# Half the staged writes, eight strided fetches a pair, and output projections behind the attention loop

## Chip, core and metric

The kernel runs on one core of one Trainium2 chip. The metric is the device time of one execution in microseconds (us), lower being better. TensorE (PE) multiplies matrices, VectorE (DVE), ScalarE (ACT) and GpSimd (POOL) work element by element, and SyncE (SP) issues the DMAs.

## What is computed

One macaron block on x of shape (2, 1024, 128), all in fp32: half of a routed feed-forward network (FFN, 8 experts of width 512, two per token), attention with 16 heads (key width 16, value width 64), and half of the FFN again, each behind a layer norm and added to x. The attention's softmax runs over the queries (axis 1), not over the keys.

```python
def _L0_attn_ref(x, query_proj, key_proj, value_proj, output_proj):
    q = jnp.einsum('bnd,hkd->bnhk', x, query_proj)
    k = jnp.einsum('bnd,hkd->bnhk', x, key_proj)
    v = jnp.einsum('bnd,hvd->bnhv', x, value_proj)
    sim = jnp.einsum('bnkh,bmhk->bnhm', q, k)
    attn = jax.nn.softmax(sim * scale, axis=1)
    o = jnp.einsum('bnhm,bmhv->bnhv', attn, v)
    return jnp.einsum('bnhv,dhv->bnd', o, output_proj)

x = x + 0.5 * _L0_ffn_ref(_layernorm(x), ...)
x = x + _L0_attn_ref(_layernorm(x), ...)
x = x + 0.5 * _L0_ffn_ref(_layernorm(x), ...)
```

`_L0_ffn_ref` takes a softmax over 8 router logits, keeps the two largest, and sums gelu(x W1 + b1) W2 + b2 over all experts with these weights.

## The kernel before

The 2048 tokens lie as 16 tiles of 128, in four groups of four tiles. Each engine has its own instruction list, written by hand; semaphores join them. For precision most matmuls take operands split in a high and a low part (three matmuls for one product), the split being made by a copy and a subtraction. A matmul on plain fp32 operands is recorded as two passes in the trace.

**FFN** (`ffn_pe`, `ffn_act`, `ffn_dve`, `ffn_pool`, `ffn_sync`). All eight experts run over all tokens, in four iterations `i` of two experts; an iteration has eight units `s`, one expert and one token group each. On TensorE `hidden(i, s + 1)` (lines 358 to 360) goes ahead of `output(i, s)` (369 to 371). ACT (`front`) applies gelu, DVE (`front`) makes the high and low parts (621, 625) and evicts the output block times its gate into `ysc`, a ring of two (`back`, 648), and POOL (`add`, 481) sums it into `acc`. In the first iteration the router runs on DVE: `router()` is a generator of 20 small linked steps, some of them laid between the passes of units 2 and 3; its result is transposed by TensorE into bank 5 (399) and copied by DVE (692), and TensorE holds the fourth output block until then. In the last iteration `back_pe` (170) transposes a finished token group of `acc` back, when POOL has summed its last expert, and `residual_dve` (177) adds it to x.

**Staging** (`queries`, `values` in `att_pe`; `high_part`, `low_part`; `stage`, `load_pair` on SP). Queries and keys come out of 16 units (query or key, one of two groups of eight heads, one token group). ACT writes the high part into `sthi`, DVE the low part into `stlo`, both rings of four, and SP writes them to a DRAM buffer (823). A score matmul wants four 16-row blocks a head: query parts (high, high, low, low) against key parts (high, low, high, low). The buffer has four blocks a head, so `stage` writes each part twice, and `load_pair(k)` fetches the query and the key side of two heads with one DMA of 128 rows each (813). `high_part(n)` waits until unit n - 4 is written out. `load_pair(0)` stands on SP behind units 0 to 7.

**Attention loop** (`products`, `scores`, `maxima`, `exps`, `inverses`). 16 pairs of heads (8 for each batch), eight steps of 128 keys for each pair. A step has score matmuls (896) five heads ahead, negated maxima on DVE (1067), exponentials on ACT (1002), values scaled on POOL, and products (910) into banks 6 and 7. In the second batch's eight pairs, one of batch 0's eight output-projection tiles stands between the two halves of the first step's products: `outproj` (917) into bank 7, then `residual` on DVE (1085), and the second half waits for that. Batch 1's projections are groups 2 and 3 behind the loop, inside `first()` of the second FFN.

## Time and profile before

| | us |
|---|---|
| median of 3 runs (819.36 to 821.10) | 820.52 |
| profiled execution | 819.94 |
| its span on the core | 818.1 |
| TensorE busy | 780.2 (95%) |
| DVE busy | 677.1 (83%) |
| ACT busy | 617.4 (75%) |
| POOL busy | 202.8 (25%) |

The span is the time from the first to the last recorded instruction; the rest of the execution lies around it. A busy TensorE says only that its matmuls overlap without a gap, so the places to look at are stretches in which it waits, and work that it could be spared. The first FFN runs to about 203 us, staging to 262, the loop from there to 606, and the second FFN from there to the end.

### The profile page before, as it was taken

The numbers are of one execution on the slowest core, as the hardware profiler recorded it, in microseconds if no ns is written. First come the engines' busy times: TensorE is split into PE (matmuls) and PEld (weight loads), VectorE is DVE, ScalarE is ACT, GpSimd is POOL, SyncE is SP. The second block draws the span as 40 slices with busy tenths as digits, with TensorE's granted clock in tenths as the row PEclk, the third lists the DMA queues.
The fourth block names the chain that finished last, engine by engine and source line by source line (L and its number), as shares of the span: only waits on it lengthen the run. The fifth ranks groups of instructions, "written<-read, shape, count | busy, mean of one in ns | idle before, by whom it ended". The sixth has DMA issues, their size and how long they took to land.

```text
span 818.1 us, 11781 instructions
## 1 busy us (share of the span) xinstructions
PE 780.2 (95%) x3626; PEld 464.3 (57%) x3626; DVE 677.1 (83%) x1353; ACT 617.4 (75%) x1018; POOL 202.8 (25%) x263
## 2 busy tenths in 40 slices
PE   7999999998948999999999999999999999999996
PEld 5778888886724333333333333333349678888885
DVE  7778888878727999999999888888875878888886
ACT  4867777765725999999998888888864767777762
POOL 3116532334200111111111111211121117333322
PEclk8999999999988999999999999999999999999999
DMA  5041213110798111111311110011000042202111
GB/s 171 1 158 51 104 52 103 53 52 0 276 328 322 51 52 52 52 52 52 104 52 52 52 44 24 36 52 52 1 2 1 4 155 94 99 20 97 52 51 52
DMA packets 29509, 63.04 MB, mean 77 GB/s; under 512 B 5264, under 2 KB 10768, under 8 KB 27408
## 3 DMA queue, kind: packets, MB, share of 16 engines
q1 hardware_dynamic: 29456, 62.39, 21.7%
q8 instruction: 27, 0.44, 0.2%
q14 instruction: 26, 0.21, 0.1%
HBM read 44.42 MB, written 17.96 MB: 76 GB/s over the span
## 4 chain that ended last, share of the span: by engine, by line
PE 82%; DVE 6%; DMA 5%; SPq 3%; ACT 2%; issue 1%; POOL 1%; POOLq 0%; DVEq 0%; ACTq 0%
PE ps L910 29%; PE ps L896 10%; PE ps L358 6%; PE ps L359 6%; PE ps L360 6%; PE ps L370 6%; PE ps L369 6%; PE ps L371 6%; PE ps L917 4%; SPq L823 2%; DMA w2raw<-in_w 2%; DMA qk_parts<-stlo 2%; DVE hlo L625 2%; POOL acc L481 1%; DVE hhi L621 1%
## 5 line engine op out<-in xcount | busy, mean ns | idle before, releaser
L1067 DVE TENSOR_SCALAR_CACHE_REDUCE ef<-ps 128x1024 f32<-128x1024 f32 x256 | 308.5, 1215 | 22.8 <-PE ps L896 15.4
L1002 ACT ACTIVATE ef<-ef,nmax 128x1024 f32<-128x1024 f32 x256 | 294.4, 1150 | 26.9 <-DVE ef L1067 19.5
L910 PE MATMUL ps<-ef,vs 128*64 128x512 f32 x1024 | 249.5, 605 | 3.9 <-DVE xt L1085 3.8
L435 ACT ACTIVATE ps<-ps,b_sb 128x512 f32<-128x512 f32 x256 | 169.1, 663 | 102.5 <-PE ps L360 100.5
L625 DVE TENSOR_TENSOR hlo<-ps,hhi 128x512 fp32r<-128x512 f32 x256 | 165.5, 686 | 4.8 <-ACT ps L435 0.7
L1113 POOL TENSOR_TENSOR vs<-V,rsum 128x128 f32<-128x128 f32 x128 | 51.4, 401 | 332.8 <-DVE rsum L1073 332.8
L910 PEld LDWEIGHTS ps<-ef,vs 128*64 128x64 f32 x1024 | 62.1, 136 | 120.7 <-issue 109.4
L621 DVE CAST hhi<-ps 128x512 fp32r<-128x512 f32 x128 | 87.6, 685 | 50.0 <-ACT ps L435 50.0
L481 POOL TENSOR_TENSOR acc<-acc,ysc 128x512 f32<-128x512 f32 x56 | 72.0, 1289 | 155.4 <-DVE ysc L648 154.8
L358 PE MATMUL ps<-xhi,w1lo 128*128 128x512 f32 x256 | 103.4, 404 | 3.5 <-DVE hlo L625 3.5
L359 PE MATMUL ps<-xlo,w1hi 128*128 128x512 f32 x256 | 101.8, 398 | 0.0
L360 PE MATMUL ps<-xhi,w1hi 128*128 128x512 f32 x256 | 101.8, 397 | 0.0
L369 PE MATMUL ps<-hhi,w2lo 128*128 128x512 f32 x256 | 100.8, 394 | 0.8 <-DVE gT L692 0.8
L370 PE MATMUL ps<-hlo,w2hi 128*128 128x512 f32 x256 | 100.2, 391 | 0.0
L371 PE MATMUL ps<-hhi,w2hi 128*128 128x512 f32 x256 | 99.8, 390 | 0.0
L896 PEld LDWEIGHTS ps<-qs,ks 64*128 64x128 f32 x512 | 38.6, 184 | 105.1 <-DVE ef L1067 96.2
L896 PE MATMUL ps<-qs,ks 64*128 64x512 f32 x512 | 94.9, 444 | 1.9 <-DVE ef L1067 1.9
L434 ACT ACTIVATE hhi<-ps,b_sb 128x512 fp32r<-128x512 f32 x128 | 88.6, 692 | 6.2 <-PE ps L360 1.5
L358 PEld LDWEIGHTS ps<-xhi,w1lo 128*128 128x128 f32 x256 | 48.5, 190 | 18.6 <-DVE hlo L625 7.0
L360 PEld LDWEIGHTS ps<-xhi,w1hi 128*128 128x128 f32 x256 | 48.5, 189 | 11.9
L369 PEld LDWEIGHTS ps<-hhi,w2lo 128*128 128x128 f32 x256 | 48.0, 188 | 12.2 <-DVE gT L692 1.5
L359 PEld LDWEIGHTS ps<-xlo,w1hi 128*128 128x128 f32 x256 | 48.5, 190 | 10.8
(95 smaller groups left out, 675.3 us busy)
## 6 DMA issues: line engine op xcount, KB each, us to landing
gb<-gates SPq DMA_DIRECT2D x16, 1024.0 KB, 4.6
qk_parts<-sthi SPq DMA_DIRECT2D x32, 256.0 KB, 3.6
qk_parts<-stlo SPq DMA_DIRECT2D x32, 256.0 KB, 3.9
qs<-qk_parts SPq DMA_DIRECT2D x16, 512.0 KB, 4.2
ks<-qk_parts SPq DMA_DIRECT2D x16, 512.0 KB, 5.2
w1raw<-in_w SPq DMA_DIRECT2D x16, 256.0 KB, 5.1
w2raw<-in_w SPq DMA_DIRECT2D x16, 256.0 KB, 5.5
xt<-in_x SPq DMA_DIRECT2D x4, 256.0 KB, 4.5
```

The lines of the kernel that those rows point to most:

```text
L358: nc.tensor.matmul(bank(mc), w1lo[:, u, w], xhi[:, cols], start=True, stop=False)
L359: nc.tensor.matmul(bank(mc), w1hi[:, u, w], xlo[:, cols], start=False, stop=False)
L360: nc.tensor.matmul(bank(mc), w1hi[:, u, w], xhi[:, cols], start=False, stop=True).then_inc(F.h, 1)
L369: nc.tensor.matmul(y, w2lo[:, u, w], hhi[:, s % 2, mc, :], start=(mc == 0), stop=False)
L370: nc.tensor.matmul(y, w2hi[:, u, w], hlo[:, s % 2, mc, :], start=False, stop=False)
L371: last = nc.tensor.matmul(y, w2hi[:, u, w], hhi[:, s % 2, mc, :], start=False, stop=(mc == MC - 1))
L435: nc.scalar.activation(bank(mc), bank(mc), ACT.Gelu, bias=b1_sb[:, u, mc:mc + 1]).then_inc(F.gelu, 1)
L625: nc.vector.tensor_tensor(hlo[:, s % 2, mc, :], bank(mc), hhi[:, s % 2, mc, :].bitcast(F32), ALU.subtract).then_inc(F.lo, 1)
L896: last = nc.tensor.matmul(bank(slot_bank(u) + half), ks[rows, k % 2, m * P:(m + 1) * P], qs[rows, k % 2, half * 512:(half + 1) * 512], sta ...
L910: last = nc.tensor.matmul(bank(6 + half)[x * VD:(x + 1) * VD, :], vs[:, t % VRING, x * VD:(x + 1) * VD], ef[:, (2 * t + x) % ERING, half * ...
L1002: nc.scalar.activation(ef[:, c, :], ef[:, c, :], ACT.Exp, scale=-1.0, bias=nmax[:, c:c + 1], accum_out=esum[:, c:c + 1]).then_inc(s_exp, 1)
L1067: nc.vector.tensor_scalar(ef[:, c, :], bank(slot_bank(u), 2), -1.0, None, ALU.mult, ALU.min, accum_out=nmax[:, c:c + 1]).then_inc(s_max, 1)
```

## The change

1. **Staging.** The DRAM buffer holds two blocks a head instead of four; each part is written once, and the copy is made by the fetch: `load_pair` issues eight DMAs of 32 rows, each into every fourth partition, instead of two of 128 rows. `load_pair(0)` moves behind units 8 and 9, and the written-out semaphores are kept for each batch apart.
2. **Output projections.** Batch 0's tiles leave the loop and become groups 0 and 1 behind it, in banks 4 and 5. Their residuals and statistics move there too.
3. **Ends of the last expert.** DVE evicts output blocks 1, 2 and 3 one unit earlier. In the first FFN, the forward transpose of group 0 goes ahead of the last output block on TensorE.
4. **Router.** Links are laid into unit 3 alone; unit 2 goes ahead of them, one eviction between them, and ACT does unit 3 ahead of the exponential.
5. **Last sum.** For the last token group TensorE adds `acc` and `ysc` in PSUM (`finish_pe`) instead of POOL.

```diff
-        qkd = nc.dram_tensor("qk_parts", [2, H, KD, 4, TOK], F32, kind="Internal").ap()
+        qkd = nc.dram_tensor("qk_parts", [2, H, KD, 2, TOK], F32, kind="Internal").ap()
...
+        def finish_pe(pe, n, g):
+            F = ffns[1]
+            pe.wait_ge(F.acc, A0 + GR * (E - 3) + g + 1)
+            for t in range(TPG):
+                at = (g * TPG + t) * P
+                nc.tensor.matmul(bank(back_bank(n, g))[:, t * P:(t + 1) * P], acc[:, at:at + P], ident, start=True, stop=False)
+                if t == 0:
+                    pe.wait_ge(F.scaled, S0 + GR * E)
+                last = nc.tensor.matmul(bank(back_bank(n, g))[:, t * P:(t + 1) * P], ysc[:, (2 * GR - 1) % 2, t * P:(t + 1) * P],
+                                        ident, start=False, stop=True)
+            last.then_inc(n.back, 1)
...
             def first():
-                forward_pe(pe, n, 0)
-                forward_pe(pe, n, 1)
                 if outproj:
+                    outproj(0)
+                    outproj(1)
+                    forward_pe(pe, n, 0)
+                    pe.wait_ge(n.res, 1)
                     outproj(2)
+                    forward_pe(pe, n, 1)
+                    pe.wait_ge(n.res, 2)
...
                 hidden(0, 0)
                 if outproj:
-                    pe.wait_ge(n.res, 1)
+                    pe.wait_ge(n.res, 3)
                     outproj(3)
...
                     output(i, s)
+                if F.after.k == 1:
+                    forward_pe(pe, F.after, 0)
                 output(i, 2 * GR - 1)
...
                 front(0, 2)
+                front(0, 3)
                 act.wait_ge(F.sh, 1)
                 nc.scalar.activation(ex[:, :, :], pr[:, :, :], ACT.Exp).then_inc(F.ex, 1)
...
                 low_dve(dve, n, 3)
+                front(0, 2)
                 gates = router()
                 for _ in range(3):
                     next(gates)
-                front(0, 2, gates, 2)
                 front(0, 3, gates, 2)
+                back(0, 0)
                 for _ in gates:
                     pass
-                back(0, 0)
                 back(0, 1)
...
                 front(i, 3)
                 back(i, 0)
+                back(i, 1)
                 front(i, 4)
-                back(i, 1)
-                front(i, 5)
                 back(i, 2)
                 back(i, 3)
+                front(i, 5)
                 back(i, 4)
...
-                    rows = qkd[what, 2 * p:2 * p + 2, :, :, cols].rearrange("h k j n -> (h k j) n")
-                    sp.dma_start(tile[:, u, :].bitcast(F32), rows).then_inc(s_pair[u], 16)
+                    for part in range(2):
+                        rows = qkd[what, 2 * p:2 * p + 2, :, part, cols].rearrange("h k n -> (h k) n")
+                        for copy in range(2):
+                            block = (2 * part + copy, 2 * copy + part)[what]
+                            sp.dma_start(tile[block:P:4, u, :].bitcast(F32), rows).then_inc(s_pair[u], 16)
...
                 for part, st in enumerate((sthi, stlo)):
-                    for copy in range(2):
-                        block = (2 * part + copy, 2 * copy + part)[what]
-                        dst = qkd[what, heads, :, block, g * 512:(g + 1) * 512].rearrange("h k n -> (h k) n")
-                        sp.dma_start(dst, st[:, n % 4, :].bitcast(F32)).then_inc(s_st[n % 4], 16)
+                    dst = qkd[what, heads, :, part, g * 512:(g + 1) * 512].rearrange("h k n -> (h k) n")
+                    sp.dma_start(dst, st[:, n % 4, :].bitcast(F32)).then_inc(s_st[n // HALF][n % 4], 16)
...
-            for n in range(half):
+            for n in range(HALF + 2):
                 stage(n)
...
                 products(t, 0)
-                k, m = divmod(t, MT)
-                if m == 0 and k >= NP:
-
-                    pe.wait_ge(s_o[0], k)
-                    pe.wait_ge(s_o[1], k)
-                    outproj(0, k - NP, bank(7)[:, 0:D]).then_inc(s_op, 1)
                 products(t, 1)
...
-                    if k >= NP - 1 and u == 2 * first_step(k + 1) + 6:
-                        residual(k - NP + 1)
-            statistics_dve(dve, norms[2], 0)
             inverses(STEPS - 1)
-            statistics_dve(dve, norms[2], 1)
             first_half(PAIRS - 1)
```

SP's list around the first fetch, before and then after: `sthi` and `stlo` are the staged parts, `qk_parts` the DRAM buffer, `qs` and `ks` the fetched pair.

```order
L823 DMA qk_parts<-sthi 128x512 [waits s_qklo]
L823 DMA qk_parts<-sthi 128x512
L823 DMA qk_parts<-stlo 128x512 x2
L813 DMA qs<-qk_parts 128x1024 [waits s_st2,s_st3,s_st1,s_st0]
L813 DMA ks<-qk_parts 128x1024
```

```order
L847 DMA qk_parts<-sthi 128x512 [waits s_qklo]
L847 DMA qk_parts<-stlo 128x512
L839 DMA qs<-qk_parts 32x1024 [waits s_st02,s_st03,s_st01,s_st00]
L839 DMA qs<-qk_parts 32x1024 x3
L839 DMA ks<-qk_parts 32x1024 x4
```

A unit's four writes have become two, and the fetch's two DMAs eight; in the second list the unit ahead of the fetch is unit 9, in the first unit 7.

TensorE's list from the loop's last products on, before and then after: `oT_b` and `wo_sb` are the projections' operands, `xn` the normalised rows to transpose, `wr_sb` the router's weights, `w1lo` the first expert's.

```order
L910 MATMUL ps<-ef,vs 64x512 x12
L188 MATMUL ps<-consts,xn 128x128 x8
L917 MATMUL ps<-wo_sb,oT_b 128x128 x32
L340 MATMUL ps<-wr_sb,xf 128x8 x8
L358 MATMUL ps<-xhi,w1lo 128x512
```

```order
L930 MATMUL ps<-ef,vs 64x512 x12
L937 MATMUL ps<-wo_sb,oT_b 128x128 x64
L200 MATMUL ps<-consts,xn 128x128 x4
L937 MATMUL ps<-wo_sb,oT_b 128x128 x32
L200 MATMUL ps<-consts,xn 128x128 x4
L350 MATMUL ps<-wr_sb,xf 128x8 x8
L368 MATMUL ps<-xhi,w1lo 128x512
```

Two projection groups (64 matmuls) now stand right behind the last products, and the two transposes have moved behind groups 1 and 2.

DVE's list in the last iteration of the second FFN, from the first eviction (`ysc`) on, before and then after; `hhi` and `hlo` are a unit's parts.

```order
L648 SCALAR_TENSOR_TENSOR ysc<-ps,b_sb,gb 128x512
L621 CAST hhi<-ps 128x512
L625 TENSOR_TENSOR hlo<-ps,hhi 128x512
L621 CAST hhi<-ps 128x512
L625 TENSOR_TENSOR hlo<-ps,hhi 128x512 x3
```

```order
L668 SCALAR_TENSOR_TENSOR ysc<-ps,b_sb,gb 128x512 x2
L641 CAST hhi<-ps 128x512
L645 TENSOR_TENSOR hlo<-ps,hhi 128x512
L641 CAST hhi<-ps 128x512
L645 TENSOR_TENSOR hlo<-ps,hhi 128x512 x3
```

The second block's eviction has moved from behind unit 4's passes to ahead of them; the same has been done to blocks 2 and 3 at unit 5.

## Rows read from the trace of the kernel before

**Rows 1.** The page's chain that ended last: share of the span by engine.

```profile
PE 82%; DVE 6%; DMA 5%; SPq 3%; ACT 2%; issue 1%; POOL 1%; POOLq 0%; DVEq 0%; ACTq 0%
```

**Rows 2.** Windows: busy us of PE, PEld, DVE, ACT, POOL; clock; DMA; GB/s.

```profile
223.60:254.60 31.00, 18.84 (x61) 11.76 (x59) 9.28 (x14) 8.85 (x16) 0.00 (x0) 0.83 0.96 352
...
240.00:250.00 10.00, 5.33 (x12) 3.64 (x12) 2.67 (x4) 2.28 (x4) 0.00 (x0) 0.53 1.05 403
...
262.90:424.90 162.00, 162.00 (x771) 50.36 (x770) 158.77 (x329) 158.66 (x266) 25.68 (x64) 1.00 0.18 60
```

**Rows 3.** Timeline, ACT in the staging: start, us, instruction, [idle before <-releaser].

```profile
242.22 0.60 ACT L982 ACTIVATE sthi<-ps 128x512 fp32r<-128x512 f32 x1 [7.99 <-DMA qk_parts<-stlo]
```

**Rows 4.** Timeline, SP issues: a bias; staged writes, queue free and full.

```profile
48.61 0.44 SPq L280 DMA_DIRECT2D b_sb<-in_b  x1
...
208.95 0.81 SPq L823 DMA_DIRECT2D qk_parts<-sthi  x2
...
247.45 1.34 SPq L823 DMA_DIRECT2D qk_parts<-stlo  x2
```

**Rows 5.** Timeline, TensorE from staging unit 8 to the first scores (L896).

```profile
223.60 0.39 PE L858 MATMUL ps<-xhi,wqklo 128*128 128x512 f32 x1
...
223.83 0.40 PE L859 MATMUL ps<-xlo,wqkhi 128*128 128x512 f32 x1
...
254.62 0.74 PE L896 MATMUL ps<-qs,ks 64*128 64x512 f32 x4
```

**Rows 6.** The pair fetches' line: issue ns min/median/max, start; then landing.

```profile
L813 SPq DMA_DIRECT2D ks<-qk_parts x16: 433/433/1894, 233.5 to 555.4; - x16
...
DMA to landing us min/median/max: 3.8/5.0/6.1
```

**Rows 7.** The staged writes' line: from issue to landing.

```profile
DMA to landing us min/median/max: 2.1/3.7/6.5
```

**Rows 8.** Chain in order of time, first loop step with a projection (L917) inside.

```profile
424.92 1.01 PE ps L910 x4
425.93 2.00 PE ps L917 x16
...
430.12 1.87 PE ps L910 x8
```

**Rows 9.** Timeline, TensorE: last products, first projection group, second hidden unit.

```profile
600.76 5.70 PE L910 MATMUL ps<-ef,vs 128*64 128x512 f32 x24
...
608.93 7.31 PE L917 MATMUL ps<-wo_sb,oT_b 128*128 128x128 f32 x64
...
628.16 0.48 PE L358 MATMUL ps<-xhi,w1lo 128*128 128x512 f32 x1
```

**Rows 10.** Timelines and group of lines, ends of the last experts.

```profile
190.58 0.66 PE L170 MATMUL ps<-consts,acc 128*128 128x128 f32 x4 [1.66 <-POOL acc L481]
...
799.66 0.66 PE L170 MATMUL ps<-consts,acc 128*128 128x128 f32 x4 [1.65 <-POOL acc L481]
...
795.84 3.77 POOL L481 TENSOR_TENSOR acc<-acc,ysc 128x512 f32<-128x512 f32 x3 [4.19 <-DVE ysc L648]
...
791.17 0.69 DVE L621 CAST hhi<-ps 128x512 fp32r<-128x512 f32 x1 [0.89 <-ACT ps L435]
...
L648 DVE SCALAR_TENSOR_TENSOR ysc<-ps,b_sb,gb 128x512 f32<-128x512 f32 x48 | 35.6, 744 | 5.8 <-PE ps L371 4.0 <-POOL acc L481 1.7
```

**Rows 11.** Timelines, TensorE and DVE around the second FFN's router.

```profile
643.88 0.50 PE L358 MATMUL ps<-xhi,w1lo 128*128 128x512 f32 x1 [1.22 <-DVE hlo L625]
...
653.15 0.49 PE L369 MATMUL ps<-hhi,w2lo 128*128 128x512 f32 x1 [0.39 <-DVE gT L692]
...
649.02 0.37 DVE L614 SCALAR_TENSOR_TENSOR gte<-gw,col 128x128 f32<-128x128 f32 x1
...
639.78 0.68 DVE L621 CAST hhi<-ps 128x512 fp32r<-128x512 f32 x1
```

**Rows 12.** Timeline, POOL's last addition.

```profile
812.68 1.26 POOL L481 TENSOR_TENSOR acc<-acc,ysc 128x512 f32<-128x512 f32 x1 [1.43 <-DVE ysc L648]
```

More of the change, by code:

```diff
@@ L171, in back_pe @@
             last.then_inc(n.back, 1)
+        def finish_pe(pe, n, g):
[9 more added lines that the diff above has]
+            last.then_inc(n.back, 1)
         def residual_dve(dve, n, g):
-            dve.wait_ge(n.back, g - 1 if n.k == 2 else g + 1)
+            dve.wait_ge(n.back, g + 1)
             xg = xt[:, g * TPG:(g + 1) * TPG, :]
@@ L207, in statistics_dve @@
                 dve.wait_ge(s_x[g], 16)
-            elif n.k == 2 and g < 2:
-                dve.wait_ge(s_res, TPG * (g + 1))
             else:
-                dve.wait_ge(n.res, g - 1 if n.k == 2 else g + 1)
+                dve.wait_ge(n.res, g + 1)
             for t in range(g * TPG, (g + 1) * TPG):
@@ L453, in first @@
                 front(0, 2)
+                front(0, 3)
                 act.wait_ge(F.sh, 1)
                 nc.scalar.activation(ex[:, :, :], pr[:, :, :], ACT.Exp).then_inc(F.ex, 1)
-                for s in range(2, 2 * GR):
+                for s in range(3, 2 * GR):
                     front(0, s + 1)
@@ L527, in last @@
             def last(i):
-                for s in range(2 * GR):
+                for s in range(2 * GR - F.f):
                     add(i, s)
@@ L748, in macaron_kernel @@
         s_qklo = sem("s_qklo")
-        s_st = [sem(f"s_st{u}") for u in range(4)]
+        s_st = [[sem(f"s_st{b}{u}") for u in range(4)] for b in range(B)]
         s_v = sem("s_v")
@@ L819, in stage @@
                 for part, st in enumerate((sthi, stlo)):
-                    for copy in range(2):
-                        block = (2 * part + copy, 2 * copy + part)[what]
-                        dst = qkd[what, heads, :, block, g * 512:(g + 1) * 512].rearrange("h k n -> (h k) n")
-                        sp.dma_start(dst, st[:, n % 4, :].bitcast(F32)).then_inc(s_st[n % 4], 16)
-            half = len(UNITS) // B
-            for n in range(half):
+                    dst = qkd[what, heads, :, part, g * 512:(g + 1) * 512].rearrange("h k n -> (h k) n")
+                    sp.dma_start(dst, st[:, n % 4, :].bitcast(F32)).then_inc(s_st[n // HALF][n % 4], 16)
+            for n in range(HALF + 2):
                 stage(n)
             for u in range(4):
-                sp.wait_ge(s_st[u], ST * half // 4)
+                sp.wait_ge(s_st[0][u], ST * HALF // 4)
             load_pair(0)
-            for n in range(half, len(UNITS)):
+            for n in range(HALF + 2, len(UNITS)):
                 stage(n)
@@ L906, in products @@
                     pe.wait_ge(s_o[half], k)
-                if half == 1 and m == 0 and k >= NP:
-                    pe.wait_ge(s_res, k - NP + 1)
                 for x in range(2):
@@ L952, in att_pe @@
                 products(t, 0)
-                k, m = divmod(t, MT)
-                if m == 0 and k >= NP:
-                    pe.wait_ge(s_o[0], k)
-                    pe.wait_ge(s_o[1], k)
-                    outproj(0, k - NP, bank(7)[:, 0:D]).then_inc(s_op, 1)
                 products(t, 1)
-            pe.wait_ge(s_o[0], PAIRS)
-            pe.wait_ge(s_o[1], PAIRS)
             def outproj_group(g):
+                b, j = divmod(g * TPG, MT)
+                if g == 0:
+                    pe.wait_ge(s_o[0], NP)
+                    pe.wait_ge(s_o[1], NP)
+                if g == 2:
+                    pe.wait_ge(s_o[0], PAIRS)
+                    pe.wait_ge(s_o[1], PAIRS)
                 for tt in range(TPG):
-                    last = outproj(1, (g - 2) * TPG + tt, bank(back_bank(norms[2], g))[:, tt * D:(tt + 1) * D])
+                    last = outproj(b, j + tt, bank(back_bank(norms[2], g))[:, tt * D:(tt + 1) * D])
                 last.then_inc(norms[2].back, 1)
@@ L1078, in first_half @@
                     for u in range(4):
[L1079 removed]
+                        dve.wait_ge(s_st[0][u], ST * HALF // 4)
+                        dve.wait_ge(s_st[1][u], ST * HALF // 4)
                 dve.wait_ge(s_av[0], last_step(k) + 1)
                 nc.vector.tensor_copy(oT[b][:, p, 0:512], bank(6)).then_inc(s_o[0], 1)
[L1083 to L1085 removed]
             for u in range(HEADS):
@@ L1191, in _ @@
             ffn_pe(pe, ffns[1], outproj_group)
-            for g in (2, 3):
-                back_pe(pe, norms[3], g)
+            back_pe(pe, norms[3], 2)
+            finish_pe(pe, norms[3], 3)
 def kernel(L0_attn_x, L0_attn_query_proj, L0_attn_key_proj, L0_attn_value_proj, L0_attn_output_proj,
```

34 lines of the change are left out of this document (18 added, 16 removed).

## Prediction

> **What bounds the kernel now.** I read the chain that ended last, then busy time by stretches, then the order of time around each place the diff touches. The chain is TensorE for 82% [rows 1], so a gain has to come from TensorE's work or from a stretch in which TensorE waits. The stretches show where that is [rows 2]. In 262.9 to 424.9 (the attention loop's first half) TensorE is busy for all of its 162.0 us: 64 steps of 2.53 us. DVE (158.8) and ACT (158.7) lie just beneath it. In 223.6 to 254.6 TensorE is busy for 18.8 of 31 us, while the DMA engines are at 0.96. That is the staging of query and key parts: ACT waits 7.99 us for a staging buffer to be written out [rows 3], and TensorE, idle through that wait, has a granted clock of 0.53 from 240 to 250, near its lower level (1.2 GHz against 2.4). The other places are short stops of 0.4 to 1.7 us, and the output projections inside the loop's second half.
>
> **Staging.** Before, each of 16 units writes its high and low part twice: 64 writes of 256 KB. When the queue is full, a pair of them takes 1.34 us to issue; free, it takes 0.81 [rows 4], so about 0.4 us is an issue's own cost and 0.67 the transfer's. After, 32 writes remain, 1.34 us of transfer a unit. TensorE's pitch is 0.23 us a matmul (223.60 to 223.83) [rows 5]; a unit there comes with two value projections, nine matmuls or 2.1 us, in the first eight units, and with one in the second eight, 1.4 us. So the writes alone would now keep up. If nothing waited, TensorE would go from unit 8 at 223.6 through 8 x 3 query matmuls and 12 value projections of 3 (60 x 0.233 = 14.0 us) to the first scores at 237.6; they stand at 254.62 [rows 5]. That is the upper end, 17.0 us. Values 24 to 27 go through two banks, each emptied by a 0.6 us copy: about 0.9 us more.
>
> What takes some of it back is the first pair's fetch. It stands on SP behind ten staged units instead of eight, and is eight DMAs instead of two. An issue costs 0.43 us for the 512 KB of a key fetch and 0.44 for a bias of 2 KB [rows 4, 6], so eight hold SP for 3.4 us, against 0.8 for two. By TensorE's pace, with 0.60 us on ACT for a high part and some 0.7 on DVE for a low one, unit 9's low part is ready at about 226.5 and unit 10's at 228.5. SP writes unit 9 until 227.5, issues the fetches until 231.0, and only then units 10 and 11, until 232.7. A staged write lands 2.1 us (least) to 3.7 us (median) after its issue [rows 7]; with a nearly empty queue I take 2.9. Unit 11 has then landed at 235.2. The buffer ring has four places, so unit 15's high part on ACT waits until then instead of starting at 233.5; behind it on ACT is the copy of value 22, for which value 24 on TensorE waits. Value 24 starts at about 236.5 instead of 234.8, and the first scores at 239.5. **Gain 254.62 - 239.5 = 15.1 us**, with 14.3 and 16.1 as the ends from the landing time and from no wait. From these scores to the loop's first product runs the same chain of maxima, exponentials and value copies as before.
>
> The loop's other fetches are 14 pairs of eight DMAs, each pair asked for 20.2 us (8 x 2.53) ahead. Issue is 3.4 us, and today's fetch of 512 KB lands in 5.0 us [rows 6]: nothing waits for them. That cover is gone only if a pair takes over 20.2 us.
>
> **Loop.** Each of eight pairs loses the 16 projection passes (eight fp32 matmuls, each recorded twice) between the halves of its first products. The step from 424.92 should end at 427.45; the next products start at 430.12 [rows 8]: 2.67 us a pair, projection (2.00) and the wait for the DVE residual in one. TensorE was the bound there and stays it, at 2.53 us a step as in the first half. **Gain 8 x 2.67 = 21.4 us.**
>
> **Behind the loop.** The projections come back as two groups of 64 passes at 7.14 us (608.93 to 616.07 by the next row's start) [rows 9]. Before, TensorE's last product is issued at 600.76 + 24 x 0.233 = 606.3 and the second hidden unit begins at 628.16 [rows 9]: 21.9 us, of which about 2 are waits for copies and the normalised rows. After, it begins group 0 at once. Its sequence up to the same hidden unit is four groups (28.6), three transposes (1.05), 16 router matmuls (1.7), one hidden unit (2.85): 34.2 us. The change adds waits on TensorE for residuals 0 and 1, behind which everything queues. Residual 0, statistics, POOL's rstd and scaling (some 4.7 us) must fit under group 1's 7.14 us, and do. Residual 1 has group 2 as cover. Only the second router group waits, 0.1 us for ACT's copy, since its transposes now stand right ahead of it. So 34.3 - 21.9: **cost 12.4 us**.
>
> **Ends of the last expert, both FFNs.** TensorE waits 1.66 us at 190.58 and 1.65 at 799.66 for POOL's sum of block 4, the last expert's first [rows 10]. POOL does three sums in a row from 795.84 since DVE evicts blocks 2, 3 and 4 together. After, blocks 1, 2 and 3 are evicted a unit earlier. DVE is idle for 0.89 us before unit 5's first cast at 791.17, which takes one more eviction (0.74); the two now ahead of it end at about 790.9. The sum wanted is then ready 0.4 us before TensorE asks. **Gain 3.3 us.** In the first FFN the forward transpose moves ahead of the last output block: DVE's eviction of that block is then late instead, so 0.1 us remains.
>
> **Router.** TensorE waits 1.22 us at 643.88 and some 0.3 more right behind it, since router links stretch DVE's third unit [rows 11]. After, that unit is free of them and the stop goes, but the fourth takes them, and cannot start until its own inputs come from ACT, at 643.3. From there the unit with its twelve links takes 6.7 us, as the third did from its first cast at 639.78, and one eviction and the last five links 2 us: gates at 652.0 (649.4 before [rows 11]), against TensorE's arrival at 650.3. TensorE now waits there for what it lost before, and the next output block starts at 652.95 instead of 653.15 [rows 11]. **Gain 0.2 us, twice.** On ACT the exponential with its two table loads goes behind the fourth unit; the fifth starts 1.1 us later there, under TensorE's wait.
>
> **Last sum.** POOL's last addition (1.26 us [rows 12]) and its hand-overs go; TensorE does seven 128-column matmuls of two passes (0.112 each, as in the projections) behind the last eviction instead of four transposes (0.66). 1.26 + 0.08 + 0.66 against 0.06 + 1.56 + 0.17: **gain 0.2 to 0.3 us.**
>
> **Sum.** Against the profiled execution's 819.94 (span 818.1; the runs' median is 820.52, 0.6 above): -15.1 - 21.4 + 12.4 - 3.3 - 0.1 - 0.4 - 0.3 = -28.2, **791.7 us**. The staging end points, a unit of waiting behind the loop and 1 us of doubt on the rest give 789.5 to 794.3.
>
> **Rivals.** (1) The fetches run in series. Then each lasts at least a landing: 2.1 us at least for 256 KB [rows 7], 16.8 us a pair. In the loop that still hides under 20.2. For the first pair it does not: landed at 244.4, units 10 and 11 behind it in the queue at about 247, scores at 252. Staging keeps 2.6 us of its gain: 804.2; half overlapped, 796 to 800. Against it, staged writes are issued 0.67 us apart and land after 3.7, so several are in flight. The Trainium skill (DMA: Bandwidth & Descriptors, Rules for kernel authors) speaks against this edit: it says that transfers to disjoint sets of partitions serialize, and to use one 128-partition transfer. By the same page's fit for DMAs issued by GpSimd (Anatomy of one DMA: 2.0 us plus bytes over 436 GB/s, an estimate of 2.3 us a fetch), in series, the sum would be some 806. The trace shows no fetch of 32 partitions; of overlap between transfers it shows more than that sentence grants, though from one tile each.
>
> (2) Slower: the same series, but a fetch of over 2.53 us. Then every pair of the loop is late. With today's least landing of a fetch, 3.8 us [rows 6], a pair takes 30.4 us, 10.2 too many, 14 times: about 947. It eats the whole gain from 2.67 us a fetch. For it: that is under the landing of any fetch shown. Against it: it wants no overlap at all.
>
> (3) Something waits behind the loop or the sums at the expert ends come too late (margin 0.4 us): 1 to 3 us in each place, 794.3 to 797.
>
> (4) More: no wait in the staging ring and the router stops gone (1.5 us each): 786.8 to 789.5.
>
> **How the numbers follow.** Forecast 0.70, (1) 0.13, (2) 0.02, (3) 0.08, (4) 0.07. A range of 788.0 to 797.5 holds the forecast, (3), and parts of (1) and (4). A measurement can tell about 0.2%, 1.6 us, from no change; nothing but (2) and a pile-up of small losses ends there or above: faster 0.97, same 0.01, slower 0.02.
>
> **What would show it.** Right: first scores some 15 us sooner after unit 8, the granted clock at 1.00 all through staging, DMA share well under 0.96; loop steps of 2.53 us in both halves; about 34 us from the last product to the second hidden unit; no POOL wait on TensorE at the expert ends; a wait for the gates of about 2 us before the fourth output block. Wrong: ACT waiting several us for staged writes at units 14 and 15, scores waiting for fetches, or a loop step over 2.53.

## Result and profile after

The changed kernel takes 798.89 us (median of four runs, 796.27 to 799.09), the kernel before 820.57 beside it: ratio 0.9732, 95% interval 0.9712 to 0.9753. That is faster, by 21.7 us; the forecast was 28.2 less, and 798.89 lies 1.4 us above the range. The profiled run of after is 799.08 with a span of 797.3, so 20.8 us of span have to be accounted for.

The engines' busy time and the chain that ended last, from the page of after (against [rows 1]):

```profile
PE 776.5 (97%) x3638; PEld 467.6 (59%) x3638; DVE 676.5 (85%) x1347; ACT 615.9 (77%) x1018; POOL 201.3 (25%) x262
...
PE 89%; DVE 5%; DMA 2%; ACT 1%; SPq 1%; issue 1%; POOL 0%; DVEq 0%; ACTq 0%
```

TensorE's share of the chain went from 82% to 89%, and DMA's from 5% to 2%. Cutting both timelines at the same eight instructions of TensorE gives the ledger (us; "first scores" is the first score matmul, "last products" the block of 24 of [rows 9]):

| stretch | before | after | change | forecast |
|---|---|---|---|---|
| start to first query matmul | 204.68 | 202.66 | -2.0 | -1.95 |
| staging, to first scores | 49.94 | 39.52 | **-10.4** | -15.1 |
| to first products | 8.31 | 8.29 | 0 | 0 |
| loop, to last products | 337.83 | 318.25 | **-19.6** | -21.4 |
| to second hidden unit | 27.40 | 40.19 | +12.8 | +12.4 |
| to the hidden unit behind the gates' block | 27.85 | 28.87 | **+1.0** | -0.2 |
| to the third token group's transpose back | 155.64 | 153.22 | -2.4 | -1.65 |
| to the end | 6.46 | 6.28 | -0.18 | -0.3 |

Three lines fell short: staging by 4.7, the loop by 1.8, the router by 1.2. The other lines came within 0.8 of the forecast. The first line's agreement is partly luck: kernels of the next section whose instruction lists are the same up to there took 201.28 us (three DMAs a pair) to 205.01 (TensorE's stops filled), as the clock fell less or more.

**Staging.** SP's timeline of after, from the last write of unit 9 (start, us, instruction; against [rows 4]):

```profile
225.44 0.66 SPq L847 DMA_DIRECT2D qk_parts<-stlo  x1
226.29 2.46 SPq L839 DMA_DIRECT2D qs<-qk_parts  x4
228.79 2.51 SPq L839 DMA_DIRECT2D ks<-qk_parts  x4
231.34 0.58 SPq L847 DMA_DIRECT2D qk_parts<-sthi  x1
...
232.97 0.43 SPq L847 DMA_DIRECT2D qk_parts<-stlo  x1
```

The eight fetches hold SP from 226.29 to 231.30, 5.0 us and not 3.4; units 10 and 11 are written only behind them, until 233.4. ACT's timeline shows who waits for that (in brackets: idle before, and what ended it; against [rows 3]):

```profile
234.92 0.60 ACT L1001 ACTIVATE sthi<-ps 128x512 fp32r<-128x512 f32 x1 [4.85 <-DMA qk_parts<-stlo]
236.37 0.60 ACT L1001 ACTIVATE sthi<-ps 128x512 fp32r<-128x512 f32 x1 [0.86 <-DMA qk_parts<-stlo]
236.87 0.59 ACT L995 ACTIVATE V<-ps 128x512 f32<-128x512 f32 x1
```

The high parts of units 14 and 15 wait for the ring places of units 10 and 11, and the copy of value 22 stands behind them on ACT. TensorE's timeline, value 24, the first scores and the loop's first two product groups (against [rows 5]):

```profile
237.60 0.76 PE L903 MATMUL ps<-wvhi,xlo 128*128 128x512 f32 x1 [4.69 <-ACT V L995]
...
242.18 0.73 PE L918 MATMUL ps<-qs,ks 64*128 64x512 f32 x4
...
250.47 3.49 PE L930 MATMUL ps<-ef,vs 128*64 128x512 f32 x8
...
254.64 1.94 PE L930 MATMUL ps<-ef,vs 128*64 128x512 f32 x8
```

Value 24 waits 4.69 us for that copy. The four values from there take 4.6 us to the first scores instead of the 3.0 forecast: at the end of the idle stretch and behind it the clock is low. Windows of PE (busy us, granted clock, DMA share, GB/s; against [rows 2]), the last one in the loop:

```profile
236.00:240.00 4.00, 2.40 (x6) 0.63 1.02 381
...
250.40:254.00 3.60, 3.60 (x11) 0.54 0.00 0
```

**Loop.** The steps are 2.53 us in both halves, with two exceptions. The first step of all takes 4.17 (250.47 to 254.64) at a granted clock of 0.54, near the lower of the two levels. Right ahead of it TensorE stops twice:

```profile
248.75 0.46 PE L918 MATMUL ps<-qs,ks 64*128 64x512 f32 x1 [1.35 <-DVE ef L1087]
249.81 0.73 PE L918 MATMUL ps<-qs,ks 64*128 64x512 f32 x3 [0.59 <-DVE ef L1087]
```

The same two stops stand in the trace of before, where the clock did not fall behind them and the first products took 1.94 us:

```profile
262.26 0.73 PE L896 MATMUL ps<-qs,ks 64*128 64x512 f32 x3 [0.59 <-DVE ef L1067]
262.93 1.94 PE L910 MATMUL ps<-ef,vs 128*64 128x512 f32 x8
```

The fall costs 1.64 us (4.17 against 2.53). The other exception, a step at 494.99, is 0.36 longer, and before had one 0.2 longer: -21.4 - 0.2 + 1.64 + 0.36 = -19.6.

**Router.** The gates' transpose and the fourth output block in the second FFN of after (against [rows 11]):

```profile
632.86 0.39 PE L416 MATMUL ps<-consts,gte 128*128 128x128 f32 x1 [1.52 <-DVE gte L634]
633.63 0.80 PE L379 MATMUL ps<-hhi,w2lo 128*128 128x512 f32 x1 [0.38 <-DVE gT L716]
634.23 0.63 PE L380 MATMUL ps<-hlo,w2hi 128*128 128x512 f32 x1
...
637.09 0.39 PE L379 MATMUL ps<-hhi,w2lo 128*128 128x512 f32 x1
```

The wait is 1.9 us (about 2 forecast), and counted from the second hidden unit the block starts 0.27 us sooner (0.2 forecast). But its first six matmuls stand 0.43 us apart where 0.23 is usual: the granted clock is 0.50 in 633.2 to 636.2, so it fell here too. From the last hidden unit ahead of the gates to the next behind them this trace has 9.88 us in the second FFN and 8.57 in the first.

### The profile page after: what moved, and what is told of

Read it like the earlier page. It is cut to its first block, busy times and chain, and to the rows that moved or that the text cites. A ratio compares the mean times of both kernels' runs of the same rounds, so it can differ in the third digit from the quotient of the medians.

```text
span 797.3 us, 11852 instructions
## 1 busy us (share of the span) xinstructions
PE 776.5 (97%) x3638; PEld 467.6 (59%) x3638; DVE 676.5 (85%) x1347; ACT 615.9 (77%) x1018; POOL 201.3 (25%) x262
## 4 chain that ended last, share of the span: by engine, by line
PE 89%; DVE 5%; DMA 2%; ACT 1%; SPq 1%; issue 1%; POOL 0%; DVEq 0%; ACTq 0%
PE ps L930 29%; PE ps L918 10%; PE ps L368 7%; PE ps L369 7%; PE ps L379 7%; PE ps L370 7%; PE ps L380 7%; PE ps L381 7%; PE ps L937 4%; DMA w2raw<-in_w 1%; PE ps L350 1%; DVE hlo L645 1%; ACT ef L1021 1%; DMA xt<-in_x 1%; PE ps L903 1%
```

## Experiments

Each kernel differs from the changed one by the edit of which the main lines are shown. "Staging stretch" is from the first query matmul to the first scores: 49.94 us before, 39.52 after.

### The fetch in another place

```diff
-            for n in range(HALF + 2):
+            for n in range(HALF + 4):
                 stage(n)
...
-            for n in range(HALF + 2, len(UNITS)):
+            for n in range(HALF + 4, len(UNITS)):
```

> The first pair's eight fetches stand on SP behind staged unit 11 instead of unit 9; nothing else differs from the changed kernel. Theory A (the eight issues, 5.0 us of SP, hold up the writes of units 10 and 11, for whose ring places ACT waits 4.85 and 0.86 us): both writes go out by about 231, ACT's waits fall under 2 us, value 24 on TensorE starts at about 235 instead of 237.60. The fetches are then issued from 231 to 236 and land at about 238.6, so the first scores come at 238.7 to 239.5 instead of 242.18: 2.7 to 3.5 us less, about 795.5 to 796.3. Rival B (the transfers themselves are the limit: 341 GB/s and a DMA share of 0.98 in 232.7 to 242.3): the same bytes in another order save nothing, and scores wait for fetches issued 5 us later, some 244 to 247: 799 to 804.

Measured: 793.61 us (792.00 to 794.87), 5.3 less than the changed kernel; ratio to before 0.9671 (0.9650 to 0.9693) instead of 0.9732. Staging stretch 33.69. SP's timeline, the fetches:

```profile
230.52 2.52 SPq L839 DMA_DIRECT2D qs<-qk_parts  x4
233.09 2.50 SPq L839 DMA_DIRECT2D ks<-qk_parts  x4
```

TensorE's timeline, the first scores and the loop's first two product groups:

```profile
237.96 0.73 PE L918 MATMUL ps<-qs,ks 64*128 64x512 f32 x4
...
246.24 3.49 PE L930 MATMUL ps<-ef,vs 128*64 128x512 f32 x8
...
250.42 1.94 PE L930 MATMUL ps<-ef,vs 128*64 128x512 f32 x8
```

A window up to the first scores (busy us of PE, PEld, DVE, ACT, POOL, then clock, DMA share, GB/s):

```profile
232.70:238.00 5.30, 5.21 (x22) 3.12 (x20) 2.77 (x4) 2.75 (x5) 0.00 (x0) 1.00 0.77 244
```

The issues cost the same 5.0 us, but nobody waits for what is behind them: no wait of ACT for a ring place is left, and TensorE is busy for 5.21 of 5.30 us at full clock up to the first scores. The gain is 5.8 us in the stretch, larger than expected. Counted from the first query matmul, value 24 starts 4.6 us sooner (30.3 us against 34.9; 2.6 expected), since no wait is left at all, and from there to the first scores it is 3.4 us instead of 4.6, since the clock stays up. The clock goes with the stop: in the twelve traces in which TensorE stops for several us in staging the granted clock falls to 0.50 there, and in the two without such a stop (this one and the last kernel below) it does not. The same bytes moved, so rival B falls. The loop's first step still takes 4.18 us.

### Fewer and other DMAs for a pair

Six DMAs: the query side as two of 64 rows.

```diff
+                for copy in range(2):
+                    rows = qkd[0, 2 * p:2 * p + 2, :, :, cols].rearrange("h k q n -> (h k q) n")
+                    sp.dma_start(qs[copy:P:2, u, :].bitcast(F32), rows).then_inc(s_pair[u], 16)
```

> The query side of a pair comes by two DMAs of 64 rows into every second partition, the key side by four of 32 rows as in the changed kernel; the bytes and the place behind unit 9 are the same. If an issue into strided partitions costs 0.6 us whatever its rows: six take 3.7 us instead of 5.0, units 10 and 11 are written 1.3 us sooner, and the first scores come 1.3 us sooner after the first query matmul (38.2 instead of 39.5). If it goes by rows or bytes: a 64-row issue takes 1.2 us, the six take 5.0, and nothing moves.

Measured: 798.18 us in one run; staging stretch 38.65, 0.9 sooner instead of 1.3. The first pair's six issues take 3.7 us (226.19 to 229.90). The line of each side in that kernel (issue ns, least, median, most):

```profile
L840 SPq DMA_DIRECT2D ks<-qk_parts x64: 593/594/724, 227.4 to 530.2; - x64
L836 SPq DMA_DIRECT2D qs<-qk_parts x32: 457/596/1597, 226.2 to 527.7; - x32
```

0.594 us for 32 rows and 0.596 for 64: the price is by DMA, not by row. But with 3.7 us of issues, near the 3.4 of the forecast, the stretch is still 3.8 us over the forecast's 34.8. Part of what the shorter issues save is lost behind them: unit 11's low part lands 3.6 us after its issue instead of 3.3.

Five DMAs: the query side as one DMA whose source repeats each row.

```diff
+                rows = qkd[0, 2 * p:2 * p + 2, :, :, cols].rearrange("h k q n -> (h k q) n")
+                sp.dma_start(qs[:, u, :].bitcast(F32), rows.unsqueeze(1).broadcast_to([64, 2, N])).then_inc(s_pair[u], 16)
```

> The query side of a pair comes by one DMA of 128 rows whose source repeats every row, the key side by four of 32 rows as in the changed kernel; the staged writes keep the changed kernel's form, and the fetch its place behind unit 9. In the kernel with three DMAs a pair, the staged writes' form differed too, and they landed late (median 3.8 and 5.6 us, up to 15.4, against 2.5 and 3.0). If the writes' form was to blame: five issues take about 2.9 us instead of 5.0, staged writes land as in the changed kernel, and the first scores come 2 us sooner after the first query matmul, 37.5 instead of 39.5: about 796.8. If the repeated source was: ACT waits at units 14 and 15 for more than 6 us in all and the first scores come later than 39.5.

Measured: 794.33 us in one run, in which no clock fall is seen at the loop's start or at either router; staging stretch 38.67. The issues took 3.2 us (2.9 expected), but half of what that saves was lost: unit 10's last write, issued by 229.4, lets ACT go on at 233.05 only, some 3.6 us later (2.5 in after). Its issue now starts 2.7 us before the pair's last fetch has landed, 1.4 in after. So the transfers seem to take a part once the issues are shorter; how large a part was not tried by itself.

Three DMAs, the key side repeated as well, which needs another order of rows and for that another layout of the staged query parts:

```diff
+                    if what == 0:
+                        dst = qkd[0].rearrange("h k q n -> h (k q) n")[heads, part * KD:part * KD + KD, g * 512:(g + 1) * 512]
...
+                q_rows = qkd[0].rearrange("h k q n -> (h k q) n")[2 * p * 32:(2 * p + 2) * 32, cols]
+                sp.dma_start(qs[:, u, :].bitcast(F32), q_rows.unsqueeze(1).broadcast_to([64, 2, N])).then_inc(s_pair[u], 16)
+                for h in range(2):
+                    k_rows = qkd[1, 2 * p + h, :, :, cols].rearrange("k q n -> (k q) n")
+                    sp.dma_start(ks[64 * h:64 * h + 64, u, :].bitcast(F32),
+                                 k_rows.unsqueeze(0).broadcast_to([2, 32, N])).then_inc(s_pair[u], 16)
```

> A pair is fetched by three DMAs instead of eight, with the same bytes: the query side by one of 128 rows whose source repeats every row, the key side by one of 64 rows for each head, also repeated in the source; the rows of a head are put in another order on both sides. It still stands behind unit 9. Theory A (number of issues): three issues at 0.43 to 0.62 us are 1.3 to 1.9 us instead of 5.0; units 10 and 11 are written at their own pace, value 24 starts at about 234.5, the first scores at 237.3 to 238.5 instead of 242.18: 793.7 to 795.3. Rival B (bytes): no issue count matters, DMA share in the stall stays at 0.98, within 1 us of 798.9.

Measured: 810.75 us (807.99 to 813.55), staging stretch 52.14, far outside both expectations. One wait on ACT there:

```profile
245.94 0.60 ACT L1003 ACTIVATE sthi<-ps 128x512 fp32r<-128x512 f32 x1 [11.36 <-DMA qk_parts<-stlo]
```

The three issues were short (medians 0.54 us for the query side and 0.49 for each half of the key side; 2.3 us in all for the first pair), yet the staged writes took 0.8 to 0.9 us to issue (medians) and up to 15.4 to land. The edit had changed the writes' form with the fetch. The next kernel keeps that form and fetches by eight DMAs of 32 rows without a repeated source:

```diff
+                for h in range(2):
+                    q_rows = qkd[0, 2 * p + h, :, :, cols].rearrange("k q n -> (k q) n")
+                    for copy in range(2):
+                        sp.dma_start(qs[64 * h + copy:64 * h + 64:2, u, :].bitcast(F32), q_rows).then_inc(s_pair[u], 16)
...
+                        sp.dma_start(ks[64 * h + 32 * copy:64 * h + 32 * copy + 32, u, :].bitcast(F32), k_rows).then_inc(s_pair[u], 16)
```

> The staged writes take the form of the kernel with three DMAs a pair (the query side in the DRAM buffer by head, part, row instead of head, row, part), and a pair is fetched by eight DMAs of 32 rows without a repeated source: the query side's into every second partition, the key side's into 32 adjacent ones. If that form of the writes made the kernel with three DMAs slow: writes land later than in the changed kernel (medians over 3.5 us against 2.5 and 3.0), ACT waits over 6 us in all for ring places at units 10 to 15, and the first scores come over 45 us after the first query matmul instead of 39.5. If the repeated source did: the writes land as in the changed kernel, and the scores come at 39 to 40. For the issue's cost: if the stride over partitions makes it 0.59 us, the key side's four take 0.43 us each, 1.7 in all; if 0.59 is the price of any such DMA, 2.4 to 2.5 in all, as the query side's.

Measured: 802.42 us in one run, staging stretch 44.66. The view of the DRAM buffer: its fetches' issues, and who waited for it (us, times):

```profile
L837 SPq DMA_DIRECT2D qs<-qk_parts x64: 447/594/1323, 228.6 to 533.9; - x64
L841 SPq DMA_DIRECT2D ks<-qk_parts x64: 302/422/1243, 232.3 to 536.1; - x64
...
  ACT sthi L1005: 12.5, 7
```

The staged writes' landing, from the page:

```profile
qk_parts<-sthi SPq DMA_DIRECT2D x16, 256.0 KB, 4.1
qk_parts<-stlo SPq DMA_DIRECT2D x16, 256.0 KB, 4.6
```

Both medians need care: the trace records no landing for the query units' writes in the new form, so they are those of the eight key units' writes, whose form is the old one (2.7 and 3.2 us for the same units in after). What the new form does is seen in the DMA engines. Windows of 256 KB query writes alone, in after and then in this kernel (clock, DMA share, GB/s):

```profile
208.00:209.00 1.00, 1.00 1.03 385
```

```profile
209.00:210.50 1.50, 1.00 0.50 162
```

And one of the kernel with three DMAs, in which only the second pair's key side is left to fetch:

```profile
256.00:261.00 5.00, 1.00 0.13 48
```

A half and an eighth of 16 engines are eight and two. Eight and two are also the outermost counts of these access patterns: eight heads in the new form of a query write, two copies in `broadcast_to([2, 32, N])`. That this count decides how many engines work is argued from these two patterns; no run varies it alone.

So two things follow for three DMAs a pair, 12.6 us worse in staging than the changed kernel. The writes' form, with the fetch of this last kernel, accounts for 5.1 of them. The other 7.5 are put down to the key side's two fetches, by the shares and not by a run of its own: at 48 GB/s the 512 KB would take some 11 us (an estimate), and the writes of units 10 and 11, issued right behind them, have landed only at 245.9 and 247.1, when ACT goes on. A repeated source as such is not to blame: the query side repeated, in the kernel with five DMAs, had none of this.

The issue's price is settled: in this kernel 32 rows into adjacent partitions take 0.42 us, into every second 0.59, and into every fourth it was 0.59. **The stride is what the prediction's 0.43 lacked.**

### TensorE's stops filled

Seven matmuls of 512 columns into bank 6, five ahead of the loop and two between its first scores:

```diff
+                        if half == 0 and fill and u == heads[-1]:
+                            for r in range(fill):
+                                nc.tensor.matmul(bank(6), wqkhi[:, 0:P], xhi[:, 0:512], start=True, stop=True)
...
+            for r in range(5):
+                nc.tensor.matmul(bank(6), wqkhi[:, 0:P], xhi[:, 0:512], start=True, stop=True)
             for t in range(STEPS):
-                scores([2 * t + LEAD, 2 * t + LEAD + 1])
+                scores([2 * t + LEAD, 2 * t + LEAD + 1], 2 if t == 0 else 0)
```

> Seven matmuls more, into a bank that is overwritten afterwards, fill TensorE's two stops (1.35 and 0.59 us) right ahead of the loop's first products; nothing else differs from the changed kernel. In the changed kernel the granted clock of 250.4 to 254.0 is 0.54 and the first step takes 4.17 us against 2.53. Theory C (these stops, together with the idle time before, bring the clock down): with them filled the clock stays at 1.00, the first step takes 2.53 us: 1.6 us less, 797.2. Rival D (the clock there answers the 4.69 us stop at 232.9 or chance, and not these stops): the step stays at 4.17 us, 798.9.

Measured: 797.37 us (796.08 to 799.31). The trace has the first step at 2.53 us:

```profile
253.44 1.94 PE L933 MATMUL ps<-ef,vs 128*64 128x512 f32 x8
...
255.97 1.94 PE L933 MATMUL ps<-ef,vs 128*64 128x512 f32 x8
```

The median is lower by 1.5 us, as theory C has it, but the spread of the runs is larger than that, and half of the traces without these fills have a first step of 2.53 us too. This run alone does not show that the fills did it.

Seven into bank 4 around the gates' transpose (`FILL` is 5):

```diff
+                pe.wait_ge(F.scaled, S0 + 1)
+                for r in range(FILL):
+                    nc.tensor.matmul(bank(4), w1hi[:, 0, 0:P], xhi[:, 0:512], start=True, stop=True)
                 pe.wait_ge(F.g, 1)
...
+                for r in range(2):
+                    nc.tensor.matmul(bank(4), w1hi[:, 0, 0:P], xhi[:, 0:512], start=True, stop=True)
                 pe.wait_ge(F.gTs, 1)
```

> Seven matmuls more, into a bank that is overwritten afterwards, fill TensorE's wait for the gates (1.52 and 0.38 us) ahead of the fourth output block, in both FFNs; nothing else differs from the changed kernel. In the second FFN six matmuls behind that wait go at the lower clock (0.43 us each against 0.23). Theory C: with the wait filled the clock stays up, 1.2 us less in the second FFN, 797.7; if the fill ends late it costs up to 0.3 us in each. Rival D: no change, 798.9 to 799.5.

Measured: 797.89 us (797.23 to 800.18). Both router passages take 8.6 us; the loop's first step, not filled here, takes 4.09. The median is 1.0 us below the changed kernel's, within the spread of the runs.

### Parts undone

The staging part undone (the lines of item 1 of the change back in their old form):

```diff
-            for n in range(HALF + 2):
+            for n in range(half):
                 stage(n)
...
+                    sp.dma_start(tile[:, u, :].bitcast(F32), rows).then_inc(s_pair[u], 16)
```

> The staging part alone undone in the changed kernel: four writes a unit, a fetch of two DMAs behind unit 7, as before; all other parts stay. Theory: the stretch from the first query matmul to the first scores goes back from 39.5 to 49.9 us, and the loop's first step from 4.17 to 2.53 since before its clock did not fall there: +10.4 - 1.6 = +8.8, 807.7. Rival (the part's worth reaches beyond that stretch, over less DMA traffic in the loop): over 809.

Measured: 808.73 us (806.57 to 814.54), 9.8 more. Staging stretch 49.96, as before. The first loop step stays at 4.16 us, though staging is as before: what was expected of it there was wrong.

The output projections undone:

```diff
                 products(t, 0)
+                k, m = divmod(t, MT)
+                if m == 0 and k >= NP:
+                    pe.wait_ge(s_o[0], k)
+                    pe.wait_ge(s_o[1], k)
+                    outproj(0, k - NP, bank(7)[:, 0:D]).then_inc(s_op, 1)
                 products(t, 1)
...
+                    if k >= NP - 1 and u == 2 * first_step(k + 1) + 6:
+                        residual(k - NP + 1)
```

> The output projections alone undone in the changed kernel: batch 0's tiles are back in the loop with their residuals. Theory, from the two traces: +21.5 us in the loop's second half, -12.8 behind it: +8.7, 807.6. Rival (the prediction's own terms): +21.4 - 12.4 = +9.0, 807.9; the two are told apart by the stretches only. Over 810 or under 805 would say that the projections' place is worth something elsewhere as well.

Measured: 806.29 us (805.75 to 807.81), 7.4 more. By the stretches: loop 337.83, 19.58 more than in after, whose own loop holds 2.0 of clock fall and one long step, so 21.6; behind the loop 27.39, 12.80 less. Both terms are close to the prediction's (21.4 and 12.4).

The ends of the last expert undone:

```diff
-                if F.after.k == 1:
-                    forward_pe(pe, F.after, 0)
...
                 back(i, 0)
-                back(i, 1)
                 front(i, 4)
+                back(i, 1)
+                front(i, 5)
                 back(i, 2)
                 back(i, 3)
-                front(i, 5)
```

> DVE's and TensorE's order at the last expert's end alone undone, in both FFNs. Prediction's term: 1.66 + 1.65 us of waiting for POOL come back, and 0.1 for the forward transpose: 802.3. By the two traces, the unit there goes from 6.0 back to 7.9 us, twice 1.88: 802.6. Rival (the wait was covered by something else and moves): under 800.

Measured: 800.37 us (799.39 to 803.10), 1.5 more. Both waits are back in its trace:

```profile
191.56 0.66 PE L170 MATMUL ps<-consts,acc 128*128 128x128 f32 x4 [1.66 <-POOL acc L499]
...
783.02 0.66 PE L170 MATMUL ps<-consts,acc 128*128 128x128 f32 x4 [1.64 <-POOL acc L499]
```

The unit there takes 7.86 and 7.84 us instead of 6.01 and 5.98, 3.7 in all. The medians show less than half of it: four runs a side, with clock falls of 1 to 3 us among them, do not resolve it.

The router's order undone:

```diff
                 front(0, 2)
-                front(0, 3)
                 act.wait_ge(F.sh, 1)
...
-                front(0, 2)
                 gates = router()
                 for _ in range(3):
                     next(gates)
+                front(0, 2, gates, 2)
                 front(0, 3, gates, 2)
-                back(0, 0)
```

> The router's order alone undone in the changed kernel (links laid into units 2 and 3, as before). Rival (the prediction's term, 0.2 us for each of two routers): 0.4 us slower, 799.3. Theory C: in one piece the stop for the gates (1.52 and 0.38 us) lets the clock fall in 8 of the 14 router passages traced so far without a fill, for 1.3 to 2.5 us each; with the stop in four pieces, the longest 1.22 us, it did not fall in the two passages of the kernel before. Then undoing it gives up 0.4 to 0.6 us and saves some 1.7 on the mean: 797.2 to 798.2, with no step of over 8.2 us at either router in the trace.

Measured: 799.99 us (798.55 to 800.64), 1.1 more and not 0.7 to 1.7 less. In its trace neither router shows a fall, as theory C said, but the kernel is not faster. The medians do not resolve the edit's worth, but a stretch does: from the second hidden unit to the one behind the gates' block the second FFN takes 27.87 us here (27.85 before), 27.6 in traces of the changed order where the clock holds, and 28.8 to 29.2 where it falls. The edit gains 0.3 us in the first case (0.2 forecast) and loses 1.0 to 1.3 in the second.

### All that helped, together

The fetch behind unit 11 and both fills:

> The first pair's fetch behind staged unit 11, and fills (seven matmuls each, into banks that are overwritten) in TensorE's stops ahead of the loop's first products and ahead of the fourth output block of both FFNs. Theory: the three terms add up: with the fetch moved alone the median was 793.61; the loop's first step loses 1.65 us of lower clock (4.18 us against 2.53), which goes; the steps behind the gates, which take 9.9 to 11.1 us where the clock falls and 8.6 where it does not, take 8.6 in both FFNs, 0 to 1.3 us each on the mean of runs: 790.0 to 792.0. Rival: the clock falls elsewhere instead (it has to rest somewhere): within 0.5 us of 793.6.

Measured: 790.50 us (789.42 to 791.98), ratio to before 0.9638 (0.9625 to 0.9651), 8.4 less than the changed kernel. Its first scores, first products, the next ones, and the fourth output block of the second FFN:

```profile
235.94 0.73 PE L927 MATMUL ps<-qs,ks 64*128 64x512 f32 x4
...
244.42 1.94 PE L939 MATMUL ps<-ef,vs 128*64 128x512 f32 x8
...
246.95 1.94 PE L939 MATMUL ps<-ef,vs 128*64 128x512 f32 x8
...
625.93 0.50 PE L380 MATMUL ps<-hhi,w2lo 128*128 128x512 f32 x1
```

By the traces: staging stretch 33.73 (5.8 less), first step 2.53 (1.64 less), second router 8.63 (1.25 less), against 0.2 more between first scores and first products for the fill: 8.5 in all. TensorE is busy for 99% of the span. From 19 us, behind the start, to 788 the granted clock is 1.00 (window: clock, DMA share, GB/s):

```profile
19.00:788.00 769.00, 1.00 0.20 67
```

The other runs agree: the mean clock over the span is 0.996 to 0.998 in all five, against 0.989 to 0.994 in the four with the fetch moved alone. So the rival, a fall elsewhere instead, is not what came.

## Why the prediction was wrong

**Direction right, and most mechanisms.** The loop's projections (21.6 by the undone kernel against 21.4), the stretch behind the loop (12.8 against 12.4; 34.6 us from the last product's issue to the second hidden unit), the waits for POOL (gone in both FFNs, 3.7 against 3.3), the shape of the router's wait (1.9 us ahead of the fourth block) and the last sum (0.2 against 0.3) came out as worked out or nearly so.

**The step that failed is what the first pair's fetch takes back.** The forecast had the fetch hold up value 24 by 1.7 us (236.5 instead of 234.8); it costs 4.6. Counted from the first query matmul, value 24 starts at 34.9 us, where the forecast had 31.8: 3.1 late. With the fetch moved out of the way it starts at 30.3, where the forecast had 30.1 without any wait. The prediction's own sign of being wrong, ACT waiting several us at units 14 and 15, is what came.

The chain is the forecast's, link by link: fetches, then units 10 and 11, then ACT's wait for unit 11's place, the copy of value 22, value 24. The sizes are not. "An issue costs 0.43 us for the 512 KB of a key fetch and 0.44 for a bias of 2 KB" took its rows from DMAs into adjacent partitions, and the new ones go into every fourth: 0.594 us each, 5.0 for eight with the gaps instead of 3.4. That is 1.6 of the 3.1 us. The fetch starts 0.8 late (23.6 against 22.8), and the rest lies in the writes behind it and the high part. The price alone would not have saved the forecast: with 3.7 and 3.2 us of issues the stretch was still 38.65 and 38.67, since the writes behind the fetch then landed later. The place settles it: two units further back it came to 33.69, better than the forecast's 34.8.

**The clock was left out.** The forecast had the granted clock at 1.00 all through staging and put no term for it anywhere. TensorE's idle 4.7 us brought it down, and the values behind take 4.6 us, where they take 3.4 at full clock with the fetch moved (3.0 forecast): 1.2 us. Two more falls, at the loop's start (1.64) and at the second router (1.3), stand where the trace of before has none. Of the 7.7 us by which the three lines fell short, the clock is thus 4.1 and the fetch 3.1.

**The rivals.** 798.89 lies where rival (1) had put "half overlapped", but by coincidence: the fetches did not go in series. Issued 0.6 us apart, they land 2.5 and 2.6 us after their issue (medians of 64 each on the page), several in flight at once. The rule of the Trainium skill that the prediction weighed (DMA: Bandwidth & Descriptors, Rules for kernel authors) is that two transfers to disjoint partition halves serialize, as they share the same engines. In this trace they overlap: the first pair's eight are issued within 5.0 us and each lands at most 2.8 us after its issue, so the pair is there within 7.2 us of the first issue's start; one after the other they would need some 20 (8 x 2.6).

**What stays open** is why the clock falls in one execution and not in the next. Of the twelve traces without a fill there, six have a fall at the loop's start (before has none). Behind the gates it fell in 11 of 20 router passages with the changed order and no fill, for 1.3 to 2.5 us each. With the stops filled it fell in none of two and none of four, and with the router's stop in pieces (before, and the router undone) in none of four. For the loop's fill, two traces are too few to tell it from chance; the mean clocks of the last kernel's five runs speak for the fills. A share of the 21.7 us therefore differs from run to run.

## What to carry to other kernels

When one DMA is cut into several, price the new form by a row of the same form, and where there is none, ask which queue stands behind it and what its next item is worth: here 5.0 us of issues, in front of two units' writes that a full ring waited for, cost 5.8 us on TensorE, and moving the fetch by two units gave it back. Where TensorE's stops are the last thing left, filling them with work that nobody reads can be worth more than shortening them, because the clock behind the stop is part of the stop's price: here the new router order gained 0.3 us where the clock held, and its stop was followed by a fall in 11 of 20 passages. A term below the spread of the medians is better read from a stretch between two instructions that both traces have.

## What was not expected of the hardware

- The issue of a DMA on SP takes 0.42 us into 32 adjacent partitions and 0.59 into every second or fourth, for 32 rows and for 64 alike (0.594 and 0.596).
- A write of 256 KB kept the DMA share at 1.03 (385 GB/s) when its rows in DRAM lay at one even stride of 128, and at 0.50 (162 GB/s) when they lay as 8 runs of 16. Fetches whose source repeats a block of 32 rows twice ran at 0.13 (48 GB/s), and writes issued right behind them landed up to 15.4 us after their issue.
- Two stops of 1.35 and 0.59 us in an otherwise busy TensorE were followed by a granted clock near the lower level in half of the traces (the eight products behind them took 3.49 us instead of 1.94 in after). With seven matmuls in their place (1.41 and 0.74 us), which put the first products off by 0.2 us, it did not fall in the two traces that have them, too few to exclude chance.
